# Second layer of a four-layer network: forty-two in-place additions handed from VectorE to GpSimd

## What is computed

```python
xa = _ln(x, ln1_w, ln1_b)
sx = concatenate([state_row, xa[:, :-1]], axis=1) - xa
xxx = xa + sx * maa_x
t = tanh(xxx @ maa_w1).reshape(B, L, 5, -1)
mw, mk, mv, mr, mg = einsum('blfd,fdc->blfc', t, maa_w2)   # one (B, L, C) each
xw = xa + sx * (maa_w + mw)        # and xk, xv, xr, xg in the same way
r, k, v, g = xr @ Wr.T, xk @ Wk.T, xv @ Wv.T, silu(xg @ Wg.T)
w = exp(-exp(time_decay + tanh(xw @ decay_w1) @ decay_w2))
# then, over the 256 rows: out = r.(faaaa*k*v + s);  s = k*v + w*s
```

## Time and profile before

| what | value |
|---|---|
| median of 3 runs | 3393.57 us (3386.46 to 3395.83) |
| the profiled execution | 3387.74 us, its span 3385.9 us |
| mean granted clock of PE over the span | 0.955 of full |
| busy over the span: PE, DVE, ACT, POOL | 92%, 70%, 51%, 21% |
| 1600 to 1700 us, inside the second layer: PE, DVE, ACT, POOL busy | 96.80, 98.22, 58.67, 3.90 us of 100 |
| scans of the second layer (L1822) | 64, the first at 1321.0 us, the last at 2089.4 us |

### The profile page before, as it was taken

The page is one execution under the profiler, slowest core; times in us unless marked ns, Lnnn a source line. Parts: engine busy times, 40 slices in busy tenths (PEclk is TensorE's granted clock), DMA queues, the critical chain, the costliest instruction groups (busy, mean ns, idle before and its releaser), DMA issues. The chain is left out here.

```text
span 3385.9 us, 55605 instructions
## 1 busy us (share of the span) xinstructions
PE 3102.2 (92%) x20384; PEld 2385.0 (70%) x20384; DVE 2360.7 (70%) x3589; ACT 1741.1 (51%) x4185; POOL 703.0 (21%) x1207
## 2 busy tenths in 40 slices
PE   7899999999999977899999996589999999699998
PEld 6777788778877855566666653478888787588875
DVE  6776776777666755999999998267777888443212
ACT  4445555545544534455555643357777777432222
POOL 2444444454444430000000000011111111000000
PEclk9999999999999988899999997789999999899999
DMA  7668866777775655444455543300011111310004
GB/s 249 212 212 270 253 195 204 222 231 220 210 215 173 197 157 160 113 110 111 113 121 113 118 104 78 118 1 26 26 57 51 43 42 34 116 50 11 15 14 168
DMA packets 179678, 434.80 MB, mean 128 GB/s; under 512 B 52912, under 2 KB 61104, under 8 KB 154960
## 3 DMA queue, kind: packets, MB, share of 16 engines
q1 hardware_dynamic: 120256, 262.17, 27.1%
q10 hardware_dynamic: 28304, 106.09, 8.8%
q0 software_dynamic: 30848, 62.97, 7.4%
HBM read 233.95 MB, written 62.91 MB: 88 GB/s over the span
## 5 line engine op out<-in xcount | busy, mean ns | idle before, releaser
L281 POOL DMA_DIRECT2D l_probT<-l_prob x896 | 441.2, 500 | 252.5 <-DVE l_prob L783 232.8
L761 DVE TENSOR_REDUCE l_nmax<-l_bank 128x1 f32<-128x512 f32 x512 | 316.9, 681 | 199.2 <-PE l_bank L453 199.2
L576 ACT ACTIVATE l_prob<-l_bank,l_nmax 128x512 f32<-128x512 f32 x512 | 344.5, 688 | 151.5 <-DVE l_nmax L761 130.9
L783 DVE STREAM_TRANSPOSE l_prob<-l_prob 128x1024 f32<-128x1024 f32 x256 | 314.4, 1228 | 20.7 <-DVE l_acc L804 9.3
L419 PE MATMUL l_bank<-l_x_hi,l_w_hi 128*128 128x256 f32 x1024 | 297.5, 291 | 24.4 <-DVE l_x_lo L852 11.4
L419 PE MATMUL l_bank<-l_x_hi,l_w_lo 128*128 128x256 f32 x1024 | 290.7, 284 | 0.0
L419 PE MATMUL l_bank<-l_x_lo,l_w_hi 128*128 128x256 f32 x1024 | 290.5, 284 | 0.0
L1822 DVE TENSOR_TENSOR_SCAN l_kv<-l_wx,l_kv 128x2056 f32<-128x2056 f32 x64 | 283.9, 4436 | 3.1 <-DVE l_sxc L1943 1.5
L478 PE MATMUL l_bank<-l_probT,l_v 128*64 128x256 f32 x2048 | 248.8, 397 | 36.2 <-issue 17.1
L2396 ACT ACTIVATE l2a_sc<-l2a_sc,l2a_nmax 128x256 f32<-128x256 f32 x512 | 254.8, 508 | 41.1 <-DVE l2a_nmax L2512 41.1
L478 PEld LDWEIGHTS l_bank<-l_probT,l_v 128*64 128x64 f32 x2048 | 148.1, 142 | 131.5 <-issue 48.0
(11 more groups left out here) (348 smaller groups left out, 7998.8 us busy)
## 6 DMA issues: line engine op xcount, KB each, us to landing
l_probT<-l_prob SPq DMA_DIRECT2D x1152, 64.0 KB, 2.8
l_vb<-vd SPq DMA_DIRECT2D x64, 1024.0 KB
l_probT<-l_prob POOLq DMA_DIRECT2D x896, 64.0 KB, 2.4
l_w_hi<-kept_w_hi ACTq DMA_DIRECT2D x24, 1024.0 KB, 5.6
l_w_lo<-kept_w_lo ACTq DMA_DIRECT2D x24, 1024.0 KB, 5.9
l_wv_hi<-kept_wv_hi ACTq DMA_DIRECT2D x12, 1024.0 KB, 8.5
l_wv_lo<-kept_wv_lo ACTq DMA_DIRECT2D x12, 1024.0 KB, 9.3
kept_w_hi<-l_w_hi SPq DMA_DIRECT2D x8, 1024.0 KB, 10.0
```

Of the source, the lines that this page charges most:

```text
L281: eng.dma_start(probT[i % RING][r * SQ:(r + 1) * SQ, g, :, :, :, :], prob[i % RING][g * SQ:(g + 1) * SQ, r * IT:(r + 1) * IT, :, :, :]).th ...
L576: act.activation(prob[i % RING][:, :, it % 2, h, :].rearrange("p (q t) s -> p t q s", q=Q), s.ap[:, :].rearrange("p (t q s) -> p t q s", t ...
L761: dve.tensor_reduce(nmax[:, n % 2, it, h:h + 1], s.ap[:, :], AX.X, ALU.max, negate=True).then_inc(max_ready, 1)
L783: dve.transpose(own, own).then_inc(turned, 1)
```

## The change

For batch 0 (`p == 0`) nothing changes. For batches 1 to 7 DVE no longer does the additions of xa: `first_input` is called only for batch 0, and `mix` returns after the multiplication. POOL gets a function `add_rows`, which waits for ACT's half (x) or DVE's product (the others), does the same addition in place, and counts up the same `xf_ready`. Its six calls are put between POOL's other steps of the round in the order x, v, (csd), g, (nrs), w, k, (sd), r, (add_out).

```diff
+                def add_rows(p, n):
+                    i = INPUTS.index(n)
+                    to = xf[i % 2]
+                    if i:
+                        pool.wait_ge(xf_part, (len(INPUTS) - 1) * p + i)
+                    else:
+                        pool.wait_ge(x0_half, p + 1)
+                    pool.tensor_tensor(to[:, :, :], to[:, :, :], xa[:, :, 1:ROWS + 1], ALU.add).then_inc(xf_ready, 1)
+
                 for b in ALL:
+                    p = b + 1 if 0 < b + 1 < B else None
+                    if p:
+                        add_rows(p, "x")
+                        add_rows(p, "v")
                     if b >= 1:
                         deviations(csd, cdev_in, cdev_ready, b - 1)
+                    if p:
+                        add_rows(p, "g")
                     if b + 2 < B:
                         pool.wait_ge(nvar_ready, b + 2)
                         pool.tensor_tensor(nrs[:, :], nrs[:, :], power[:, :], ALU.pow).then_inc(nrs_ready, 1)
+                    if p:
+                        add_rows(p, "w")
+                        add_rows(p, "k")
+                    if b + 2 < B:
                         deviations(sd, dev_in, dev_ready, b + 1)
+                    if p:
+                        add_rows(p, "r")
                     if b >= 1:
                         add_out(b - 1)
@@ mix, on DVE
                     dve.tensor_tensor(to[:, :, :], to[:, :, :], sx[:, :, :], ALU.mult).then_inc(xf_part, 1)
+                    if p:
+                        return
                     dve.wait_ge(xf_part, (len(INPUTS) - 1) * p + i)
                     dve.tensor_tensor(to[:, :, :], to[:, :, :], xa[:, :, 1:ROWS + 1], ALU.add).then_inc(xf_ready, 1)
@@ the main loop on DVE
-                        if n == 1 and 0 <= p < B:
+                        if n == 1 and p == 0:
                             first_input(p)
```

## The result

The changed kernel takes 3473.6 us (median of 5 runs, 3464.8 to 3481.5). Its ratio to the kernel before is 1.0247, 95% interval 1.0228 to 1.0265: slower by 2.5%, where 1.5% was forecast (3443 us, range 3415 to 3475). The direction was as forecast, and so was what one addition costs DVE when it stops it; but what was to be lost by lateness was costed far too low. The size was too small by 30 us, and 1.0247 x 3393.6 us = 3477 us lies just outside the range. Of the five runs of the kernel before that were taken beside these, one lasted 5738.9 us and is left out of the ratio; the others took 3386.5 to 3395.8 us. The profiled execution took 3464.8 us, span 3463.0 us, 77 us more than the one of before, where the sum said 49.

What follows compares the result with a forecast made beforehand. DVE was taken to bound the second layer. Six rounds at 7.25 us (2.7 for x, 4.55 for five blocked additions) plus 5.6 us for round 0 gave +49 us: 3437 us profiled, 3443 us median (+1.5%), range 3415 to 3475.

Steps and rivals of the forecast that it cites:

- lateness: Second layer: late x costs 2.7 us a round at scale_y; later results cost nothing beyond the DVE shift.
- the sum: Second layer: 7.25 us in each of rounds 1 to 6, 5.6 us in round 0, none in round 7; +49 us.
- DVE sets the pace, and what it saves is 8.0 us a round: Second layer: DVE runs without holes, PE has some 3 us slack; six additions removed save DVE 8.0 us a round.
- that rival: Second layer: POOL's additions slip beside DVE's without loss, PE becomes the bound; 14 us won, 3380 us, chance 0.06.
- A POOL addition stops a two-input DVE instruction for 2.16 us: After each mix step: DVE stands 2.16 us and saves 1.25 us, +0.91 us, five times a round, +4.55 us.
- POOL waits for the instruction in flight, but gets in between two that follow each other densely: DVE's dense row: POOL's v addition waits 2.2 us for the running receive, then takes its turn while scan stands.
- Forecast for v: Mix step v, scan standing for POOL's addition: DVE loses 2.16 us and gains 1.25 us, +0.91 us a round.
- PE is then 1 us late behind v, and nothing more is lost: At project v: PE held about 1 us more, 3.7 us late as DVE is; both move together, no further loss.
- The first input costs 2.7 us a round: Input x: xf ready at 1636.6 instead of 1633.93, so first, spread_rs and scale_y run 2.7 us late.
- The PE rival: Second layer: PE's granted clock falls by 0.06, 6 us more a round, 42 us in all, 3485 us; chance 0.12.

Runs made afterwards that it cites:

- reading and lateness taken away: Changed kernel with two DVE waits for its own last product added and POOL's additions cut to two elements a partition: 3371.0 us, ratio 0.9943.
- w, k and r: Kernel before with only the additions of w, k and r moved to POOL, x, v and g on DVE: 3408.6 us, ratio 1.0055.
- The holes: Changed kernel plus DVE waits for its own last product: two, before bonus_rk and unit 3's scan, 3445.7 us; or one, before v's multiplication, 3446.2 us.
- the control: Kernel before plus two DVE waits for its own last product, before bonus_rk and unit 3's scan, POOL as before: 3393.9 us, ratio 1.0008.
- the two-element additions: Changed kernel with POOL's 42 additions cut to two elements of a partition, all waits kept: 3389.1 us, ratio 0.9990.

## Why the prediction was off

By its own steps, each with what was measured:

- *DVE sets the pace, and what it saves is 8.0 us a round.* That DVE waited for next to nothing else left out 5.3 us at scale_y. With reading and lateness taken away the layer did get faster, but only by 0.6% (forecast for that rival 14 us, measured 19 us). DVE still waits 30 us for PE there in 1350 to 2080 us. That PE then sets the pace fits (in 1600 to 1700 us of that run PE is busy 97.75 us, DVE 94.58) and was not tested further.
- *A POOL addition stops a two-input DVE instruction for 2.16 us.* 1.98 us (scans of 6.41 against 4.43). For w, k and r the sum came out: 19 us forecast, 19 us measured. There is luck in that: with 1.98 us the sum is 0.73 x 21 = 15 us, and in that run DVE's wait for ACT ahead of `first_input` grew from 3.9 to 10.6 us, which the sum does not have. Of DVE's busy time, forecast to grow by 43 us, only 3 came, since the 42 additions stopped DVE for 54 us in all, 27 times 1.98: x, v and g read mostly beside a DVE that stood or read PSUM.
- *POOL waits for the instruction in flight, but gets in between two that follow each other densely.* This is the step that failed. It stood on the earlier trace rows, a power that got in between L1869 and L1830. But L1869 had waited for its own multiplication just before (the hole between the earlier trace rows's 1650.32 + 1.22 and 1651.57), and that hole goes with the addition that the change removes. For v in rounds 1 to 6 POOL was passed over once more, by a 4.4 us scan: a record of 8.45 us, where about 4.5 was forecast. Forecast for v 6 us, measured 29 us (0.86%). The holes, the control and the two-element additions show it.
- *PE is then 1 us late behind v, and nothing more is lost.* With v ready 4.3 us later PE stood 4.7 us, and the next in PE's list, the column variances, had no slack left: 6.0 us of DVE a round.
- *The first input costs 2.7 us a round.* 4.5 us by itself (28 us in all, forecast 17). The chain named was the right one (x, `first`, spread_rs, scale_y), and where POOL was let in `first` was 2.3 us late, less than forecast. Too small was what PE does with it: its 16 matmuls were costed at full clock, from a round that was one of two such among six, and take 1.2 us a round more than before. In one round x was passed over, and in the changed kernel in four of six (5.15 us at 1551.75, behind receive and bonus_rk; in three of the four ACT's half had also come 1.7 us later): `first` then starts 12.1 us behind the scan, against 8.8 us in the other two and 6.5 before.
- *The PE rival.* It was costed by the mean clock of two stretches of 100 us, 6 us a round, and put at 0.12. In 1350 to 2050 us the granted clock fell from 0.94 to 0.91 only, about half of the 0.06 taken. Its price came where that rival said, ahead of spread_rs, and behind v too; but the larger part of the miss is v's lateness and the wait that it opened.

The loss is 84 us by its ratio and the sum said 49. Of the 35 us between them v makes 23 and x 11; the rest is within the intervals.

What decides whether POOL is passed over stays open. v got in in round 0, where the row since DVE's last hole was three instructions long, and not in rounds 1 to 6, where it was seven. k got in in rounds 0 to 5, and not in round 6. The first line is v in round 0, the second k in round 6:

```profile
1355.55 4.14 POOL L1213 TENSOR_TENSOR l_xf<-l_xf,l_xa 128x1024 f32<-128x1024 f32 x1 [14.77 <-DVE l_xf L1888]
...
2068.70 8.45 POOL L1213 TENSOR_TENSOR l_xf<-l_xf,l_xa 128x1024 f32<-128x1024 f32 x1 [13.30 <-DVE l_xf L1888]
```

A short row since the last hole, or since the last instruction that POOL stopped, goes with getting in; but at 1663.29 x got in behind the seventh instruction too (3.50 us), so a plain count is not the whole rule. That the DVE instructions ahead have already been handed over when POOL asks would fit, and was only argued.

## What to carry to other kernels

Moving a two-input elementwise step from VectorE to GpSimd beside a VectorE row of two-input instructions did not relieve VectorE here: it cost GpSimd's reading time there (1.98 us for 128x1024, against 1.14 to 1.25 us saved). Ask then how late the result comes, not only how long it takes: in this dense row it was passed over by a 4.43 us scan, and the engines that waited for it paid. And before a row of the trace is taken as proof that two instructions were dense, look whether the first of them had just waited, above all when the change removes that wait. And before one round stands for all, look at the others: the one read here had PE at full clock, four of six had not.

## What the hardware showed that was not expected

- A GpSimd addition of two elements per partition took 6.46 us beside two dense two-input VectorE instructions, and 0.19 us with VectorE idle.
- A VectorE wait of 0.04 us, or one two instructions earlier, let GpSimd in and made the whole kernel 27 to 28 us faster.
- PE at 0.50 granted clock right after a wait of 4.46 us, on the 16 matmuls that the slowest chain needed: 6.6 us from their start to the next instruction's, instead of 3.7 at full clock. Behind waits of 2.12 us in the kernel before it was 5.4 us in four rounds and 3.7 in two.
